# Post-norm linear attention and butterfly FFN on one core: the last three x chunks transposed in another PSUM bank, three more layer norms applied by ScalarE

## Chip, core, metric

One core of a Trainium2 chip. The time is device microseconds of the one core, median of 3 runs; lower is better. The engines are named as in the profile: PE (TensorE), PEld (its weight loads), DVE (VectorE), ACT (ScalarE), POOL (GpSimd), SP (the queue that issues the DMAs).

## What is computed

Input x is 4 sequences of 1024 tokens with 128 features, float32. One transformer block in post-norm form:

```python
def layernorm(x): return (x - mean(x)) / sqrt(var(x) + 1e-5)
def fmap(t): return relu(t @ W_f + b_f)            # per head, 64x64
q, k, v = split(x @ W_qkv)                         # 16 heads of 64
q, k = fmap(q), fmap(k)
kv = einsum('bhnd,bhne->bhde', k, v)
att = einsum('bhnd,bhde->bhne', q, kv) / (einsum('bhnd,bhd->bhn', q, k.sum(n)) + 1e-6)
x = layernorm(x + att.merge_heads() @ W_out + b_out)
h = butterfly(x @ W_exp + b_exp, up_weights)       # 512 hidden, 9 stages
h = butterfly(gelu(h + up_bias), down_weights)
x = layernorm(x + h @ W_con + b_con + down_bias)
```

## The kernel before

**Tiling.** The tokens form 8 chunks n of 512 (two per sequence b, c = 0 or 1) and 32 tiles of 128 tokens. Heads go in 8 pairs of 128 features. The butterflies are linear, so they are multiplied into the weights once: the up butterfly by POOL, the down butterfly by DVE in nine steps (`down_step`, slots 1 to 10). Matrix products in fp32r are made of three, from a high and a low part of each operand (`split`, L600): ACT writes the high part (`hi`, L936), DVE the low one (`lo`, L1135).

**Order.** It is written by hand as a loop over 43 slots, the same loop on each engine. One slot in steady state, on PE: a key tile for half the heads (`project_k(kt, 0)`), one pair of attention (`add_attn`), a query step of 128 features by 512 tokens (`project_q`), the other half of the keys, a second `add_attn`, the product of keys and x (`add_kx`, L678), a second `project_q`, and now and then something more. PE in slot s uses for `add_attn` what DVE (`normalise_q`, L1267, then `qn_lo`) and ACT (`qn_hi`) made in slot s - 1. From slot 28 (NO_KEYS) no key tiles are left. Each engine takes its instructions strictly in turn and waits only on counters (semaphores) of the others.

**PSUM.** Eight banks. Three (`ring`) go round among projections, denominators (`norm`), the FFN's `up` and `down` tiles: a use waits until the use three before it has been drained. Two hold `kx_ps`, one `attn_ps`. The last two matter here. `desk` takes everything that is transposed (chunks of x: `transpose_x`; of the attention: `transpose_attn`; of the first layer norm's result: `transpose_x1`; of the FFN's result: `transpose_y`; weights) and the small products `ksum` and `head_maps`. It has one user at a time: `desk_of` numbers the uses, and PE waits with `take_desk` until the one before was read (`s_dtaken`). `spare_ps` serves the weight folding and down butterfly steps 3 to 7, is last read by step 8 in slot 10, and then is empty until the last chunk's halves in the tail (`spare_of`, `take_half`).

**x transposes.** `XT_SLOT` puts x of sequence 1 in slots 2 and 6, of sequence 2 in 10 and 14, of sequence 3 in 18 and 22, at the slot's end. ACT copies the high part from `desk` at once (`xT_hi`). DVE takes a row sum and the low part only in the next slot (`xT_lo`, L1309 and L1135), after that slot's first key drain (`k_max(kt, 0)`, L1207) and two `normalise_q`. Then come `k_sum`, `qn_lo`, `k_max(kt, 1)`, and where there is one `add_x` (L1292: attention from `desk` plus x, then statistics) or `residual` (L1301: FFN plus x1), and a second `qn_lo`. In slots 15, 19, 23, 27, ... PE transposes an attention chunk in `desk` after the slot's first `project_q`; in slots 17, 19, 25, 27, 33, 35 it ends with `head_maps` in `desk`; in slots 16, 20, 24, ... it ends with `transpose_x1`, which waits for `s_x1`.

**Layer norms.** DVE makes mean and variance, POOL adds eps and takes the power -1/2 (`rstd_of`). Then there are two ways, chosen by the slot against NO_KEYS = 28. In an earlier slot POOL also makes an offset (two more operations), and ACT applies the norm in the next slot, four activations of 128x128 (`layer_norm_apply`, L1004), between the first query copy and the second `qn_hi`. From slot 28 on DVE waits for POOL and applies it itself, four operations (`layer_norm_end`, L1285), at the end of the same slot. The first layer norm of chunk n has its statistics in slot 15 + 4n, the second of chunks 0 to 3 in slots 22, 26, 30 and 34.

```python
dve.wait_ge(s_rs[i], n + 1)                       # layer_norm_end, DVE
act.wait_ge(s_of[i], 2 * n + 2)                   # layer_norm_apply, ACT
take_desk: pe.wait_ge(s_dtaken, desk_of[use])     # PE, before any use of desk
```

Of the kernel before, what the change touches and what calls it, by code (L numbers as in the profile page):

```python
# [5 lines left out]
def postln_linear_attention_butterfly_ffn_kernel(  # L6
# [123 lines left out]


# [45 lines left out]
    for s in range(SLOTS):  # L177
        order = []
        if s in KSUM_SLOT:
            order.append(("ksum", KSUM_SLOT[s]))  # L180
        if s in ATT_T_SLOT:
            order.append(("attn", ATT_T_SLOT[s]))
        if s in YT_SLOT:
            order.append(("y", YT_SLOT[s]))
        if s in MAPS_SLOT:
            order.append(("maps", *MAPS_SLOT[s]))
        if s == BIAS_T_SLOT:
            order.append(("bias",))
# [11 lines left out]
    spare_of = {("attn", LAST, 1): 0, ("x1", LAST, 1): 1, ("y", LAST, 1): 2}  # L200
# [5 lines left out]
    with ctx:  # L206
# [190 lines left out]
        def half_bank(use):  # L397
            return desk if use[2] == 0 else spare_ps

        def half_made(use):  # L400

            return (s_dmade, desk_of[use] + 1) if use[2] == 0 else (s_smade, spare_of[use] + 1)

        def half_taken(use):
            return (s_dtaken, desk_of[use] + 1) if use[2] == 0 else (s_staken, spare_of[use] + 1)
# [107 lines left out]
        def _(pool):  # L513
# [55 lines left out]
            for s in range(SLOTS):  # L569
# [25 lines left out]
        def _(pe):  # L595
# [23 lines left out]

            def transpose_weights(grp, dst):  # L620
# [258 lines left out]
            def take_half(use):  # L879
                if use[2] == 0:  # L880
                    pe.wait_ge(s_dtaken, desk_of[use])
                elif spare_of[use]:
                    pe.wait_ge(s_staken, spare_of[use])
                else:

                    pe.wait_ge(s_dn, 3 * STAGES)

# [40 lines left out]
        def _(act):  # L928
# [47 lines left out]
            def xT_hi(b, c):  # L976
                act.wait_ge(s_dmade, desk_of["x", b, c] + 1)
# [3 lines left out]
                hi(xT_h[:, b % 2, c * CH:(c + 1) * CH], desk[:, :], s_xTh)  # L981
# [57 lines left out]
            for s in range(SLOTS):  # L1039
# [91 lines left out]
        def _(dve):  # L1131
# [203 lines left out]
            for s in range(SLOTS):  # L1335
# [140 lines left out]
```

## Time and profile before

| | us |
|---|---|
| three timed runs | 342.19, 343.95, 344.32 (median 343.95) |
| the profiled execution | 346.04 |
| its span, first to last instruction | 344.1 |
| busy in it: PE | 314.7 (91%) |
| DVE | 249.2 (72%) |
| ACT | 154.9 (45%) |
| POOL | 84.4 (25%) |

Times in rows are microseconds from the span's start in the profiled execution. A timeline row gives start, duration, engine, line, operation, the tile written and those read, and in brackets how long the engine sat idle before and whose work ended that. Matmuls are pipelined: a matmul of 512 columns is shown for 0.39 us and the next begins 0.23 us after it did, so in a row of matmuls the starts are what counts. Of the span outside the instructions nothing is shown; it is the 1.9 us between 346.04 and 344.1.

### The profile page before, as it was taken

To read this page: it belongs to the slowest core of one execution; us is meant where nothing else is said; L and a number is where in the kernel's file an instruction comes from. 1 tells how busy PE (TensorE), PEld (TensorE's weight loads), DVE (VectorE), ACT (ScalarE), POOL (GpSimd) and SP (SyncE) were. 2 spreads that over 40 slices of the span, in tenths; PEclk is the share of its full clock that TensorE was granted. 3 is DMA by queue.
4 is the path that set the end of the run, shared out by engine and by line. 5 is a ranking of instruction groups with operands and counts; after the bars stand their busy time and mean duration, and the time that the engine had idled before them with its cause. 6 is when DMAs were issued, how large, how long until landed. Compare 5 with 4: busy or idle time off the path is not lost.

```text
span 344.1 us, 5110 instructions
## 1 busy us (share of the span) xinstructions
PE 314.7 (91%) x1813; PEld 218.5 (64%) x1813; DVE 249.2 (72%) x492; ACT 154.9 (45%) x272; POOL 84.4 (25%) x94
## 2 busy tenths in 40 slices
PE   5799799999989979997999889999999798989882
PEld 5666476776757756665767667567778556554562
DVE  3569999969599988678681986489647837577555
ACT  3533235444534433544452546356746553341451
POOL 4059999950000002100200220004001101111122
PEclk9999899999999999999999999999999999999998
DMA  5994153835701900720073003800290074641002
GB/s 184 253 294 137 61 183 124 250 120 127 181 2 50 199 0 4 182 65 0 5 167 80 0 3 93 185 0 2 56 225 3 3 174 105 164 116 30 21 10 61
DMA packets 25616, 33.72 MB, mean 98 GB/s; under 512 B 4184, under 2 KB 14456, under 8 KB 25592
## 3 DMA queue, kind: packets, MB, share of 16 engines
q1 hardware_dynamic: 25432, 33.38, 37.4%
q8 instruction: 14, 0.23, 0.3%
q14 instruction: 10, 0.08, 0.1%
q10 hardware_dynamic: 160, 0.03, 0.0%
HBM read 31.04 MB, written 2.36 MB: 97 GB/s over the span
## 4 chain that ended last, share of the span: by engine, by line
PE 71%; DVE 14%; DMA 5%; issue 4%; SPq 3%; POOL 2%; ACT 1%; POOLq 0%; DVEq 0%; ACTq 0%
PE ring L600 25%; PE kx_ps L678 12%; PE attn_ps L600 7%; PE ring L774 6%; PE ring L698 4%; PE desk L609 4%; PE attn_ps L728 4%; DVE qn L1267 3%; DMA x<-_L_ffn_down_weights_dram 2%; PE desk L712 2%; DMA bf_col<-in_L_attn_b_f_dram 2%; PE desk L687 2%; DVE late L1153 2%; PE ring L658 2%; SPq L474 1%
## 5 line engine op out<-in xcount | busy, mean ns | idle before, releaser
L950 ACT ACTIVATE q<-ring,bf_col 128x512 f32<-128x512 f32 x64 | 43.7, 685 | 51.2 <-PE ring L600 50.7
L552 POOL TENSOR_TENSOR var_eps<-mean_var,ln_eps 128x4 f32<-128x4 f32 x14 | 7.1, 504 | 222.7 <-DVE mean_var L1280 222.7
L678 PE MATMUL kx_ps<-k,xs 128*128 128x512 f32 x128 | 60.1, 592 | 0.0
L936 ACT ACTIVATE qn_h<-qn 128x512 fp32r<-128x512 f32 x48 | 29.6, 625 | 32.6 <-DVE qn L1267 32.6
L1267 DVE TENSOR_TENSOR qn<-q,recips 128x512 f32<-128x512 f32 x64 | 41.1, 681 | 4.3 <-DMA recips<-recip_rows 4.3
L544 POOL TENSOR_TENSOR y<-hid,y_up 128x512 f32<-128x512 f32 x18 | 34.6, 1946 | 16.9 <-DMA hid<-in_L_ffn_up_weights_dram 15.9
L1135 DVE TENSOR_TENSOR qn_l<-qn,qn_h 128x512 fp32r<-128x512 f32 x48 | 32.2, 678 | 5.2 <-ACT qn_h L936 5.0
L1207 DVE TENSOR_TENSOR k<-ring,bf_minus 128x512 f32<-128x512 f32 x32 | 21.9, 685 | 19.1 <-PE ring L600 19.1
L600 PE MATMUL ring<-xT_h,wq_h 128*128 128x512 f32 x64 | 35.5, 555 | 0.1
L1233 DVE TENSOR_TENSOR k_total<-k_total,k 128x1024 f32<-128x1024 f32 x24 | 35.3, 1472 | 0.3
L678 PEld LDWEIGHTS kx_ps<-k,xs 128*128 128x128 f32 x128 | 23.9, 189 | 17.8 <-issue 15.4
L600 PE MATMUL ring<-wk_h,xT_h 128*128 128x512 f32 x64 | 29.6, 462 | 0.0
L943 ACT ACTIVATE k<-ring 128x512 f32<-128x512 f32 x32 | 19.1, 598 | 20.0 <-PE ring L658 20.0
L600 PE MATMUL ring<-wk_l,xT_h 128*128 128x512 f32 x64 | 25.4, 397 | 0.0
L774 PE MATMUL ring<-hid,wdn 128*128 128x512 f32 x56 | 25.4, 596 | 0.0
L600 PE MATMUL ring<-wk_h,xT_l 128*128 128x512 f32 x64 | 25.4, 396 | 0.0
L600 PE MATMUL ring<-xT_h,wq_l 128*128 128x512 f32 x64 | 25.2, 394 | 0.0
L600 PE MATMUL ring<-xT_l,wq_h 128*128 128x512 f32 x64 | 25.1, 392 | 0.0
L1013 ACT ACTIVATE hid<-ring,bup_col 128x512 f32<-128x512 f32 x28 | 19.2, 686 | 8.9 <-PE ring L600 8.8
L600 PE MATMUL attn_ps<-qn_h,m_h 128*128 128x512 f32 x48 | 20.0, 418 | 1.1 <-DVE qn_l L1135 1.1
L600 PE MATMUL attn_ps<-qn_h,m_l 128*128 128x512 f32 x48 | 18.9, 393 | 0.0
L600 PE MATMUL attn_ps<-qn_l,m_h 128*128 128x512 f32 x48 | 18.7, 391 | 0.0
(171 smaller groups left out, 573.8 us busy)
## 6 DMA issues: line engine op xcount, KB each, us to landing
recips<-recip_rows SPq DMA_DIRECT2D x64, 256.0 KB, 5.0
hid<-in_L_ffn_up_weights_dram SPq DMA_DIRECT2D x9, 512.0 KB, 4.6
x<-_L_ffn_down_weights_dram SPq DMA_DIRECT2D x9, 512.0 KB, 3.8
xs<-in_L_attn_x_dram SPq DMA_DIRECT2D x4, 512.0 KB, 6.8
out_dram<-y SPq DMA_DIRECT2D x7, 256.0 KB, 4.2
q<-in_L_attn_W_qkv_dram SPq DMA_DIRECT2D x2, 512.0 KB, 8.8
q<-in_L_attn_W_qkv_dram SPq DMA_DIRECT2D x2, 256.0 KB, 3.0
q<-in_L_attn_W_out_dram SPq DMA_DIRECT2D x2, 256.0 KB, 9.2
```

Source lines behind the costliest of these rows:

```text
L544: g.tensor_tensor(term_up[f].rearrange("p (hi j lo) -> p hi j lo", j=2, lo=lo), w[:, :, :, :, f], yv[:, :, f:f + 1, :].to_broadcast([128, ...
L600: last = t_.matmul(dst, lhsT, rhs, start=start and n == 0, stop=stop and n == len(pairs) - 1)
L678: t_.matmul(kx_ps[half], xs[b % XBUF][:, t, :], k[kt % KRING][:, half * CH:(half + 1) * CH], start=t == 0, stop=t == TILES - 1).then_inc(s ...
L774: last = t_.matmul(bank(("down", n))[:, :], wdn[:, i, :], hid[:, i, :], start=i == 0, stop=i == HT - 1)
L936: a_.activation(dst, src, ACT.Copy).then_inc(done, 1)
L943: a_.activation(k[kt % KRING][:, half * CH:(half + 1) * CH], bank(("k", kt, half))[:, :], ACT.Relu).then_inc(s_taken, 1)
L950: a_.activation(q[:, i % QRING, :], bank(("q", i))[:, :], ACT.Relu, bias=bf_col[:, :])\
L1013: a_.activation(hid[:, i, :], bank(("up", f))[:, :], ACT.Gelu, bias=bup_col[:, i:i + 1])\
L1135: v.tensor_tensor(dst, src, high.bitcast(fp32), ALU.subtract).then_inc(done, 1)
L1207: v.tensor_tensor(k[kt % KRING][:, half * CH:(half + 1) * CH].rearrange("p (h d) -> p h d", d=D), bank(("k", kt, half))[:, :].rearrange("p ...
L1233: v.tensor_tensor(k_total[:, :], k_total[:, :], k[kt % KRING][:, :], ALU.add).then_inc(s_ks, 1)
L1267: v.tensor_tensor(qn[:, a % NRING, :], q[:, a % QRING, :], recips[:, a % PAIRS // RC, a % RC, :], ALU.mult).then_inc(s_qn, 1)
```

## The change

Two parts, in one diff.

**Banks.** The transposes of x in slots 14, 18 and 22 (sequence 2's second chunk and both of sequence 3) go to `spare_ps`. They leave `desk_of`, and head `spare_of`, before the three halves of the last chunk. `half_bank`, `half_made` and `half_taken` choose by membership in `spare_of`; `take_half` moves up in the text; the first use of `spare_ps` waits for the down butterfly's last step (27 counts of `s_dn`), each later one for the reader before it. No instruction is added or dropped.

**Layer norms.** `APPLY_END = 35` takes the place of NO_KEYS: the second layer norms of chunks 2 and 3 (slots 30 and 34) and the first of chunk 4 (slot 31) now have their offset from POOL and are applied by ACT in slots 31, 35 and 32. And the two apply calls move, in every slot that has one, to behind the last `qn_hi`.

```diff
+    APPLY_END = 35
...
-        if s in XT_SLOT:
+        if s in XT_SLOT and s <= max(DOWN_STEP_SLOT):
             order.append(("x", *XT_SLOT[s]))
...
-    spare_of = {("attn", LAST, 1): 0, ("x1", LAST, 1): 1, ("y", LAST, 1): 2}
+    spare_of = {}
+    for use in [*[("x", *XT_SLOT[s]) for s in XT_SLOT if s > max(DOWN_STEP_SLOT)],
+                ("attn", LAST, 1), ("x1", LAST, 1), ("y", LAST, 1)]:
+        spare_of[use] = len(spare_of)
...
-            return desk if use[2] == 0 else spare_ps
+            return spare_ps if use in spare_of else desk
...
-                    rstd_of(0, ATT_T_SLOT[s], s < NO_KEYS)
+                    rstd_of(0, ATT_T_SLOT[s], s < APPLY_END)
...
-                    rstd_of(1, YT_SLOT[s], s < NO_KEYS)
+                    rstd_of(1, YT_SLOT[s], s < APPLY_END)
...
+            def take_half(use):
+                if use not in spare_of:
+                    pe.wait_ge(s_dtaken, desk_of[use])
+                elif spare_of[use]:
+                    pe.wait_ge(s_staken, spare_of[use])
+                else:
+
+                    pe.wait_ge(s_dn, 3 * STAGES)
...
             def transpose_x(b, c):
-                take_desk(("x", b, c))
+                use = ("x", b, c)
+                take_half(use)
                 pe.wait_ge(s_xs[b], 16)
-                transpose_tiles(desk, lambda i: xs[b % XBUF][:, QUADS * c + i, :]).then_inc(s_dmade, 1)
+                transpose_tiles(half_bank(use), lambda i: xs[b % XBUF][:, QUADS * c + i, :])\
+                    .then_inc(half_made(use)[0], 1)
...
-                if s <= NO_KEYS and s - 1 in ATT_T_SLOT:
-                    layer_norm_apply(0, ATT_T_SLOT[s - 1], x1[:, ATT_T_SLOT[s - 1] % X1BUF, :, :], s_x1)
-                if s <= NO_KEYS and s - 1 in YT_SLOT:
-                    layer_norm_apply(1, YT_SLOT[s - 1], y[:, YT_SLOT[s - 1] % 2, :, :], s_yo)
...
                 for a in split_spreads(s)[1:]:
                     qn_hi(a)
+                if s <= APPLY_END and s - 1 in ATT_T_SLOT:
+                    layer_norm_apply(0, ATT_T_SLOT[s - 1], x1[:, ATT_T_SLOT[s - 1] % X1BUF, :, :], s_x1)
+                if s <= APPLY_END and s - 1 in YT_SLOT:
+                    layer_norm_apply(1, YT_SLOT[s - 1], y[:, YT_SLOT[s - 1] % 2, :, :], s_yo)
...
-                if s in ATT_T_SLOT and s >= NO_KEYS:
+                if s in ATT_T_SLOT and s >= APPLY_END:
                     layer_norm_end(0, ATT_T_SLOT[s], x1[:, ATT_T_SLOT[s] % X1BUF, :, :], s_x1)
-                if s in YT_SLOT and s >= NO_KEYS:
+                if s in YT_SLOT and s >= APPLY_END:
                     layer_norm_end(1, YT_SLOT[s], y[:, YT_SLOT[s] % 2, :, :], s_yo)
```

`xT_hi`, `xT_lo` and `project_k` read the bank and the counters through the same three helpers.

PE, last rows of slot 14 and the first of slot 15, before (`xs` is x as loaded, `late` the finished attention; slot 18 to 19 and slot 22 to 23 read likewise):

```order
L609 MATMUL desk<-ident,xs 128x128 [waits xs_2_loaded,desk_taken]
L609 MATMUL desk<-ident,xs 128x128 x3
L600 MATMUL ring<-wk_h,xT_h 128x512 [waits ring_bank_taken]
L600 MATMUL ring<-wk_l,xT_h 128x512
L600 MATMUL ring<-wk_h,xT_l 128x512
L600 MATMUL attn_ps<-qn_h,m_h 128x512 [waits qn_lo,qn_hi,attn_copied]
L600 MATMUL attn_ps<-qn_l,m_h 128x512
L600 MATMUL attn_ps<-qn_h,m_l 128x512
L600 MATMUL ring<-xT_h,wq_h 128x512 [waits ring_bank_of_bare_k_taken]
L600 MATMUL ring<-xT_l,wq_h 128x512
L600 MATMUL ring<-xT_h,wq_l 128x512
L609 MATMUL desk<-ident,late 128x128 [waits attn_copied,desk_taken]
```

And with the change:

```order
L614 MATMUL spare_ps<-ident,xs 128x128 [waits xs_2_loaded,down_butterfly]
L614 MATMUL spare_ps<-ident,xs 128x128 x3
L605 MATMUL ring<-wk_h,xT_h 128x512 [waits ring_bank_taken]
L605 MATMUL ring<-wk_l,xT_h 128x512
L605 MATMUL ring<-wk_h,xT_l 128x512
L605 MATMUL attn_ps<-qn_h,m_h 128x512 [waits qn_lo,qn_hi,attn_copied]
L605 MATMUL attn_ps<-qn_l,m_h 128x512
L605 MATMUL attn_ps<-qn_h,m_l 128x512
L605 MATMUL ring<-xT_h,wq_h 128x512 [waits ring_bank_of_bare_k_taken]
L605 MATMUL ring<-xT_l,wq_h 128x512
L605 MATMUL ring<-xT_h,wq_l 128x512
L614 MATMUL desk<-ident,late 128x128 [waits attn_copied,desk_taken]
```

The x transposes write `spare_ps` and wait for the down butterfly; the attention's transposes stand where they stood and still wait for `desk_taken`, whose last count is now that of the bias column.

ACT, slots 31 and 32, before (first row: query copies of slot 31; `hid` the gelu of an `up` tile, `recip` the denominators of `norm`):

```order
L950 ACTIVATE q<-ring,bf_col 128x512 [waits qn_done,ring_bank_made] x2
L936 ACTIVATE qn_h<-qn 128x512 [waits attn_step_added,qn_done] x2
L1013 ACTIVATE hid<-ring,bup_col 128x512 [waits ring_bank_made]
L987 ACTIVATE recip<-ring 128x128 [waits recip_stored,ring_bank_made]
L950 ACTIVATE q<-ring,bf_col 128x512 [waits qn_done,ring_bank_made] x2
L936 ACTIVATE qn_h<-qn 128x512 [waits attn_step_added,qn_done] x2
L1013 ACTIVATE hid<-ring,bup_col 128x512 [waits ring_bank_made]
L936 ACTIVATE x1T_h<-desk 128x512 [waits ring_bank_made,desk_made]
```

And with the change (`y` is the second layer norm of chunk 2, `x` the first of chunk 4):

```order
L957 ACTIVATE q<-ring,bf_col 128x512 [waits qn_done,ring_bank_made] x2
L943 ACTIVATE qn_h<-qn 128x512 [waits attn_step_added,qn_done] x2
L1011 ACTIVATE y<-y,offset,rstd 128x128 [waits offset_1_done]
L1011 ACTIVATE y<-y,offset,rstd 128x128 x3
L1020 ACTIVATE hid<-ring,bup_col 128x512 [waits ring_bank_made]
L994 ACTIVATE recip<-ring 128x128 [waits recip_stored,ring_bank_made]
L957 ACTIVATE q<-ring,bf_col 128x512 [waits qn_done,ring_bank_made] x2
L943 ACTIVATE qn_h<-qn 128x512 [waits attn_step_added,qn_done] x2
L1011 ACTIVATE x<-x,offset,rstd 128x128 [waits offset_0_done]
L1011 ACTIVATE x<-x,offset,rstd 128x128 x3
L1020 ACTIVATE hid<-ring,bup_col 128x512 [waits ring_bank_made]
L943 ACTIVATE x1T_h<-desk 128x512 [waits ring_bank_made,desk_made]
```

Each slot has four activations more. The gelu that frees a ring bank stands behind those of `y`, and `x1T_h` behind those of `x`.

DVE, from the last `qn_l` of slot 30 to that of slot 31, before:

```order
L1135 TENSOR_TENSOR qn_l<-qn,qn_h 128x512 [waits qn_hi]
L1285 TENSOR_SCALAR y<-y,mean_var,rstd 128x128 [waits rstd_1_done]
L1285 TENSOR_SCALAR y<-y,mean_var,rstd 128x128 x3
L1267 TENSOR_TENSOR qn<-q,recips 128x512 [waits qn_lo,qn_hi,recips_of_pairs_2_loaded]
L1267 TENSOR_TENSOR qn<-q,recips 128x512 [waits qn_lo,qn_hi]
L1135 TENSOR_TENSOR qn_l<-qn,qn_h 128x512 [waits qn_hi]
L1292 TENSOR_TENSOR x<-desk,xs 128x512 [waits desk_made]
L1276 BN_STATS stats<-x 128x6 [waits desk_taken]
L1276 BN_STATS stats<-x 128x6 x3
L1278 MEMSET scratch 128x1 [waits stats_0_done]
L1280 BN_AGGR mean_var<-stats 128x2 x4
L1135 TENSOR_TENSOR qn_l<-qn,qn_h 128x512 [waits qn_hi]
```

And with the change:

```order
L1142 TENSOR_TENSOR qn_l<-qn,qn_h 128x512 [waits qn_hi]
L1274 TENSOR_TENSOR qn<-q,recips 128x512 [waits qn_lo,qn_hi,recips_of_pairs_2_loaded]
L1274 TENSOR_TENSOR qn<-q,recips 128x512 [waits qn_lo,qn_hi]
L1142 TENSOR_TENSOR qn_l<-qn,qn_h 128x512 [waits qn_hi]
L1299 TENSOR_TENSOR x<-desk,xs 128x512 [waits desk_made]
L1283 BN_STATS stats<-x 128x6 [waits desk_taken]
L1283 BN_STATS stats<-x 128x6 x3
L1285 MEMSET scratch 128x1 [waits stats_0_done]
L1287 BN_AGGR mean_var<-stats 128x2 x4
L1142 TENSOR_TENSOR qn_l<-qn,qn_h 128x512 [waits qn_hi]
```

The group of four that waited for POOL (`rstd_1_done`) is gone, and `qn` follows the last `qn_l` of the slot before directly. At the end of slots 31 and 34 such a group of four goes as well.

## Rows read from the trace of the kernel before

**Rows 1.** The page: busy us, share of the span, instructions.

```profile
PE 314.7 (91%) x1813; PEld 218.5 (64%) x1813; DVE 249.2 (72%) x492; ACT 154.9 (45%) x272; POOL 84.4 (25%) x94
```

**Rows 2.** Waits: who waited for whom: us in total, times, longest us.

```profile
PE desk L609 <- DVE xT_l L1135: 5.4, 3, 1.8
```

**Rows 3.** Timeline of PE, end of slot 14 to slot 15, and in slot 19.

```profile
122.52 0.66 PE L609 MATMUL desk<-ident,xs 128*128 128x128 f32 x4 [0.26 <-DVE y_bias L1179]
...
124.86 0.40 PE L600 MATMUL ring<-xT_h,wq_l 128*128 128x512 f32 x1
127.06 0.66 PE L609 MATMUL desk<-ident,late 128*128 128x128 f32 x4 [1.80 <-DVE xT_l L1135]
...
160.23 0.66 PE L609 MATMUL desk<-ident,late 128*128 128x128 f32 x4 [1.80 <-DVE xT_l L1135]
```

**Rows 4.** Timeline of DVE: last down step; slot 16; `add_x`, slot 19; second key drain, slot 23.

```profile
94.58 0.69 DVE L1157 TENSOR_TENSOR x<-late 128x512 f32<-128x512 f32 x1
...
132.25 0.69 DVE L1207 TENSOR_TENSOR k<-ring,bf_minus 128x512 f32<-128x512 f32 x1 [0.42 <-PE ring L600]
...
162.43 0.68 DVE L1292 TENSOR_TENSOR x<-desk,xs 128x512 f32<-128x512 f32 x1
...
200.37 0.68 DVE L1207 TENSOR_TENSOR k<-ring,bf_minus 128x512 f32<-128x512 f32 x1
```

**Rows 5.** Timeline of PE: `head_maps` of slot 19, first key tile of slot 24.

```profile
164.61 1.10 PE L712 MATMUL desk<-vo,kx 128*64 128x128 f32 x16
...
203.75 0.39 PE L600 MATMUL ring<-wk_h,xT_h 128*128 128x512 f32 x1
```

**Rows 6.** Timeline of PE, slot 28 (first row) and slots 31 to 33.

```profile
247.20 0.60 PE L609 MATMUL desk<-ident,x 128*128 128x128 f32 x4
...
269.26 0.47 PE L600 MATMUL attn_ps<-qn_h,m_h 128*128 128x512 f32 x1 [0.48 <-DVE qn_l L1135]
...
271.55 0.63 PE L609 MATMUL desk<-ident,x 128*128 128x128 f32 x4 [0.67 <-DVE x L1285]
...
274.16 0.47 PE L600 MATMUL attn_ps<-qn_h,m_h 128*128 128x512 f32 x1 [0.60 <-DVE qn_l L1135]
...
276.47 1.09 PE L712 MATMUL desk<-vo,kx 128*64 128x128 f32 x16 [0.67 <-DVE x1T_l L1135]
```

**Rows 7.** Timeline of DVE, slots 30 to 31.

```profile
261.67 0.66 DVE L1135 TENSOR_TENSOR qn_l<-qn,qn_h 128x512 fp32r<-128x512 f32 x1
263.51 1.11 DVE L1285 TENSOR_SCALAR y<-y,mean_var,rstd 128x128 f32<-128x128 f32 x4 [1.18 <-POOL rstd L558]
264.54 1.28 DVE L1267 TENSOR_TENSOR qn<-q,recips 128x512 f32<-128x512 f32 x2
```

**Rows 8.** Timeline of ACT: layer norm apply in slot 28; slots 31 and 32.

```profile
244.73 1.63 ACT L1004 ACTIVATE x<-x,offset,rstd 128x128 f32<-128x128 f32 x4
...
266.39 0.67 ACT L1013 ACTIVATE hid<-ring,bup_col 128x512 f32<-128x512 f32 x1
...
268.12 0.69 ACT L950 ACTIVATE q<-ring,bf_col 128x512 f32<-128x512 f32 x1 [0.31 <-PE ring L600]
```

**Rows 9.** Timeline of POOL: a layer norm in slot 19, one in slot 27, the starts in slots 30, 31.

```profile
164.51 0.56 POOL L552 TENSOR_TENSOR var_eps<-mean_var,ln_eps 128x4 f32<-128x4 f32 x1 [22.20 <-DVE mean_var L1280]
...
166.33 0.20 POOL L563 TENSOR_TENSOR offset<-mean_minus,rstd 128x4 f32<-128x4 f32 x1
...
238.87 0.55 POOL L552 TENSOR_TENSOR var_eps<-mean_var,ln_eps 128x4 f32<-128x4 f32 x1 [4.88 <-DVE mean_var L1280]
...
241.57 0.20 POOL L563 TENSOR_TENSOR offset<-mean_minus,rstd 128x4 f32<-128x4 f32 x1
...
261.83 0.55 POOL L552 TENSOR_TENSOR var_eps<-mean_var,ln_eps 128x4 f32<-128x4 f32 x1 [20.06 <-DVE mean_var L1280]
...
268.62 0.55 POOL L552 TENSOR_TENSOR var_eps<-mean_var,ln_eps 128x4 f32<-128x4 f32 x1 [5.14 <-DVE mean_var L1280]
```

**Rows 10.** Timeline of PE, the denominators of slot 35.

```profile
288.00 1.96 PE L698 MATMUL ring<-q,ksum_cols 128*32 128x128 f32 x64 [0.87 <-ACT q L950]
```

More of the change, by code:

```diff
@@ L397, in half_bank @@
         def half_bank(use):
-            return desk if use[2] == 0 else spare_ps
+            return spare_ps if use in spare_of else desk
         def half_made(use):
-            return (s_dmade, desk_of[use] + 1) if use[2] == 0 else (s_smade, spare_of[use] + 1)
+            return (s_smade, spare_of[use] + 1) if use in spare_of else (s_dmade, desk_of[use] + 1)
         def half_taken(use):
-            return (s_dtaken, desk_of[use] + 1) if use[2] == 0 else (s_staken, spare_of[use] + 1)
+            return (s_staken, spare_of[use] + 1) if use in spare_of else (s_dtaken, desk_of[use] + 1)
         block = ctx.enter_context(nc.Block())
@@ L643, in project_k @@
                     if b:
-                        pe.wait_ge(s_dtaken, desk_of["x", b, t // QUADS] + 1)
+                        pe.wait_ge(*half_taken(("x", b, t // QUADS)))
                     else:
@@ L877, in _ @@
                     transpose_x1(X1T_SLOT[s])
[L879 to L886, printed above, removed]
             def transpose_half(use, src):
@@ L976, in xT_hi @@
             def xT_hi(b, c):
-                act.wait_ge(s_dmade, desk_of["x", b, c] + 1)
+                act.wait_ge(*half_made(("x", b, c)))
                 if b > 1:
                     act.wait_ge(s_made, ring_of["q", STEPS * (b - 2) + PAIRS * (c + 1) - 1] + 1)
-                hi(xT_h[:, b % 2, c * CH:(c + 1) * CH], desk[:, :], s_xTh)
+                hi(xT_h[:, b % 2, c * CH:(c + 1) * CH], half_bank(("x", b, c))[:, :], s_xTh)
             def norm_eps(n):
@@ L1307, in xT_lo @@
                 dve.wait_ge(s_xTh, CHUNKS * b + c + 1)
+                src = half_bank(("x", b, c))[:, :]
                 if TILES * b >= BARE:
-                    v.reduce_sum(x_part[:, b, c:c + 1], desk[:, :], axis=mybir.AxisListType.X).then_inc(s_xpart, 1)
-                lo(xT_l[:, b % 2, c * CH:(c + 1) * CH], desk[:, :], xT_h[:, b % 2, c * CH:(c + 1) * CH], s_dtaken)
+                    v.reduce_sum(x_part[:, b, c:c + 1], src, axis=mybir.AxisListType.X).then_inc(s_xpart, 1)
+                lo(xT_l[:, b % 2, c * CH:(c + 1) * CH], src, xT_h[:, b % 2, c * CH:(c + 1) * CH],
+                   half_taken(("x", b, c))[0])
             def x1T_lo(n):
```

## Prediction

> **What bounds the kernel now.** I read the page first. PE is busy for 91% of the span, the next engine, DVE, for 72% [rows 1]: PE sets the end, and a stall is worth what PE does not do in it. Then the waits, for those of PE alone: the largest behind the start-up is `desk` waiting for `xT_l`, 5.4 us in three times of 1.8 [rows 2]. Then PE's timeline at these places. After the first query step of slot 15 the attention's transposes begin at 127.06, and the last matmul before began at 124.86; matmuls follow at 0.23 us, so PE lost 127.06 - 124.86 - 0.23 = 1.97 us [rows 3]. That is the idle time shown, 1.80, plus the 0.17 by which a matmul's shown end lies beyond the point where the next could start. Slot 19 is the same (160.23), and slot 23 is the third. The x chunk that slot 14, 18 or 22 left in `desk` waits for DVE, which reads it only after a key drain and two `qn`. Last the timeline of slots 28 to 35, where DVE applies the norms: four gaps of 0.48, 0.67, 0.60 and 0.67 in slots 31 to 33 [rows 6], each with 0.17 more, so 3.1 us in all, and one of 0.87 in slot 35 [rows 10].
>
> **Banks.** (a) Slot 14: x no longer waits for the bias column's reader, 0.26 shown [rows 3], 0.4 with the hidden part. Its new wait, the last down step, ends at 94.58 + 0.69 = 95.3 [rows 4], 27 us before PE is there: nothing.
>
> (b) Slots 15, 19 and 23: the waits for `xT_l` go, 1.97 each, for the previous use of `desk` is then read long before. What is late next is DVE. In these slots it does not stop, and its work is not shorter. It is behind PE by its own backlog, so I look at each later point where PE needs it.
>
> Slot 15: the backlog ends with slot 16's key drain, for which DVE waited 0.42 us [rows 4]. PE being 1.97 + 0.4 earlier, DVE reaches that drain about 2 us late by PE's measure, but the ring's bank is needed only three uses on, and slot 16 has no `desk` use until its end. Slot 15 keeps 2.0, and slot 14 its 0.4.
>
> Slot 19: `head_maps` wants `desk` at 164.61 [rows 5], by PE's own work 1.97 + 0.05 earlier, 162.6 (0.05: matmuls after a gap start a little slower). The bank is then held by the attention that DVE adds at 162.43 for 0.68, up to 163.11 [rows 4]; with 0.06 for the signal, 163.17. PE waits 0.6 again: 1.4 is left. This is a new wait, `desk` for L1292.
>
> Slot 23: the first bank that DVE holds is that of `k_max(kt, 1)`, free at 200.37 + 0.68 = 201.05 [rows 4]; PE wants it for the first key tile of slot 24, 203.75 [rows 5] less 2.0 = 201.75. It clears by 0.7 us: 2.0.
>
> Sum of the banks: 0.4 + 2.0 + 1.4 + 2.0 = 5.8 us. Bounds: if the same 0.6, or DVE's whole backlog up to 1.1 us, came back in slots 15 and 23 too, 3.6; if slot 19 lost nothing, 6.4.
>
> **The order of ACT.** In slots 16, 20, 24 and 28 `x1` is done one `qn_h` later, 0.6 us. The tightest is slot 28: the apply began at 244.73 and took 1.63 [rows 8], so it ended at 246.36, and will at 246.97; PE transposes from 247.20 on [rows 6]. It clears by 0.2: nothing, at worst 0.6. DVE's second `qn_l` no longer waits behind the apply, which no PE instruction is waiting for: nothing.
>
> **Layer norms.** DVE drops per norm four operations (1.11 - 0.08 overlap = 1.03) and the wait for POOL, 1.18: `qn` of slot 31 starts at 264.54 - 2.21 = 262.33, right behind the `qn_l` of 261.67 [rows 7]; slot 32 starts 4.4 earlier. ACT gets 1.6 us per norm, POOL two small operations. What becomes of PE's four gaps goes step by step.
>
> POOL's whole chain with the offset took 166.33 + 0.20 - 164.51 = 2.0 us in slot 19, where DVE sat idle, but 241.57 + 0.20 - 238.87 = 2.9 us at the end of slot 27 [rows 9], where two `qn` came right behind, as they now will in slots 30 and 31. I take 2.9.
>
> Slot 31: the offset of `y` is there at 261.83 + 2.9 = 264.7 [rows 9]. ACT has made both `qn_h` by then (two `qn` of 0.64 from 262.33 on, a copy behind each), applies `y` from 264.7 to 266.4, and only then takes the gelu, which before began at 266.39 [rows 8]: so the bank that this gelu frees is no earlier, and PE's second query step of slot 32 stays where it was. ACT copies it at 268.12 as before [rows 8], done at 268.7, then the two `qn_h` (0.57 each) to 269.9, then `x1` to 271.5. Its offset, at 268.62 - 2.3 + 2.9 = 269.2 [rows 9], is in time. PE wants `x1` at 271.55 less the gap of 0.65 before 269.26, and less its own 0.83: at 270.1 it is there and waits 1.4 us, to 271.5. So of the first two gaps nothing is left, at most 0.35 with POOL's 2.0 (then the gelu ends 0.5 earlier). This is the largest new wait: `desk` for ACT's L1011, where before it was for L1285.
>
> Slot 33: the second two gaps, 0.77 + 0.84 = 1.6, were DVE's lateness (`qn_l` at 274.16, `x1T_l` at 276.47, [rows 6]). DVE being 4.4 us earlier, `qn_l` is done by 270.5, and `x1T_l`, bound by ACT's copy of `x1`, at 273.3, while PE arrives at 274.8. They go: 1.6.
>
> Slots 34 and 35: PE's gap of 0.87 waits for ACT's copy of PE's own last query step [rows 10], and the apply of `y` stands behind that: stays. DVE's 2.2 us there are hidden by its own wait for the denominators: nothing.
>
> Sum of the norms: 1.6, up to 2.0; take 1.7. Bounds: 0.6 and 3.1 (all four gaps).
>
> **A rule against it.** The chain of 2.9 beside 2.0 us [rows 9] is the one place where an added operation meets a neighbour. The Trainium skill (SBUF — State Buffer, Who interferes with whom) says that a DVE operation with two SBUF inputs and a GpSimd operation that reads SBUF block each other, the later for the whole of the other. The rows agree in direction, with 0.9 us for two `qn`; by the rule at its worst each of the three later POOL operations could wait out one. The estimate by it would be a chain of 3.8 us, `y` and with it the gelu 0.9 later, and a total of 6.6 us in place of 7.5.
>
> **Forecast.** 5.8 + 1.7 = 7.5 us. The profiled execution takes 346.04 (344.1 span, 1.94 around it, which the change doesn't touch), so it would take 338.5. The median of the runs is 343.95, 2.1 less, and where that lies no row says; none of the gaps depends on it, so I take off the same: 343.95 - 7.5 = 336.4 us. The timed runs lie 2 us apart.
>
> **Rivals.**
> 1. *DVE's backlog takes the banks' gain back.* For it: DVE is nearly without a pause in slots 15, 19 and 23, and slot 19 shows how it happens. Against: the two other places clear by 0.7 us or more. Each time 1.1 back (the larger of what slot 19 loses and DVE's backlog): 5.8 - 2.2 = 3.6, plus 1.7: 338.7.
> 2. *ACT is not in the way.* The offset comes in 2.0 us, the gelu frees its bank early, and all four gaps and slot 19's 0.6 go: 6.4 + 3.1 = 9.5, 334.4. Against: the two `qn_h` stand before the apply in ACT's row whatever POOL does.
> 3. *Part of the gaps was no loss.* PE runs ahead into the next wait (denominators, query copies by ACT) and only the norms or only the banks count: 343.95 - 1.7 = 342.2 at the least, 338.1 for the banks alone. Nothing in the rows holds PE elsewhere for 5 us.
> 4. *Slower.* The place is `x1_done`: it now comes behind both `qn_h` in slots 16, 20, 24, 28 and 32, and everything of the FFN hangs on it. If ACT started its second `qn_h` only once DVE, late in the slot, had made `qn`, PE would wait in each for what the order costs, 0.6, plus the apply, 1.6: 5 x 2.2 = 11 us lost against at most 7.5 gained, 347.4. It decides from 1.5 us per slot on. Against: slot 28, the tightest, clears by 0.2, and nowhere does `x1_done` stand in the list of PE's waits before slot 32.
>
> **Chances.** Forecast 0.66; rival 1 0.14; rival 2 0.09; rival 3 0.08 (half of it near 338, half within 1%); rival 4 0.03. A measurement of this kernel tells about 1% (3.4 us) from no change. Faster by over 1%: 0.66 + 0.14 + 0.09 + 0.04 = 0.93; within 1%: 0.04 plus 0.01 of rival 4's smaller forms, 0.05; slower: 0.02. The range runs from rival 2 to beyond rival 1, with a microsecond for the runs' scatter: 334.0 to 339.8.
>
> **What would show it.** Right: no wait of PE for `xT_l` in slots 15, 19 and 23; one of about 0.4 us shown (0.6 by starts) for L1292 before `head_maps` in slot 19; one of some 1.2 us for ACT's apply at the end of slot 32; no gap before the first attention of slot 33 or `head_maps` there; ACT's gelu of slot 31 behind the apply; a span of 336 to 337. Wrong: PE waits for `k_max` or `qn_l` in slots 16, 20 or 24; a wait for the apply in slots 16 to 28; POOL's chain above 3 us; PE as long idle as before under other names.

## The result and the profile after

| | before | with the change |
|---|---|---|
| median of the runs, us | 344.13 (342.19 to 345.81, 4 runs) | 335.31 (335.18 to 335.69, 4 runs) |
| profiled execution; its span | 346.04; 344.1 | 335.18; 333.3 |

The changed kernel takes 0.9747 of the time, 95% interval 0.9695 to 0.98: faster, 1.1 us below the forecast of 336.4 and inside its range.

The page of the changed kernel answers to [rows 1]:

```profile
PE 312.0 (94%) x1813; PEld 218.1 (65%) x1813; DVE 242.5 (73%) x480; ACT 160.1 (48%) x284; POOL 88.0 (26%) x100
```

DVE has lost the 12 operations of three norms, ACT has 12 more (5.2 us), POOL six. Of the 6.7 us that DVE is busy for less, the norms are 3.3 (its norm operations took 8.9 us before and 5.6 after); about as much is the difference between two executions, for a second trace of the kernel before has 245.7 us in place of 249.2. PE does the same 1813 matmuls and is idle for less.

PE's waits of the changed kernel, answering to [rows 2] (who waited for whom, us in total, times, longest):

```profile
PE desk L614 <- ACT x L1011: 1.4, 1, 1.4
PE desk L726 <- DVE xT_l L1142: 1.4, 1, 1.4
...
PE desk L726 <- DVE x L1299: 0.5, 1, 0.5
```

The 5.4 us for `xT_l` are gone (the 1.4 left is slot 11's, the first row of the next fence but one). Both new waits are the ones forecast: ACT's apply ahead of slot 32's transposes (1.4 us for some 1.2), and `add_x` ahead of slot 19's `head_maps` (0.5 for about 0.4).

To see where the time went I take the start of the same PE instruction in both traces. PE's timeline of the kernel before, at slots 11, 16, 27 and 36 (the other places are in [rows 5], [rows 6] and [rows 10]):

```profile
99.32 1.09 PE L712 MATMUL desk<-vo,kx 128*64 128x128 f32 x16 [1.22 <-DVE xT_l L1135]
...
132.39 1.95 PE L698 MATMUL ring<-q,ksum_cols 128*32 128x128 f32 x64 [0.17 <-ACT q L950]
...
227.44 0.66 PE L609 MATMUL desk<-ident,late 128*128 128x128 f32 x4 [0.53 <-DVE m_l L1135]
...
302.07 0.66 PE L609 MATMUL desk<-ident,late 128*128 128x128 f32 x4 [0.69 <-DVE x1T_l L1135]
```

The same instructions with the change, those of slots 19, 24, 32 and 35, and the attention's transposes of slots 15 and 23, which start without a wait now:

```profile
96.05 1.09 PE L726 MATMUL desk<-vo,kx 128*64 128x128 f32 x16 [1.36 <-DVE xT_l L1142]
...
121.49 0.60 PE L614 MATMUL desk<-ident,late 128*128 128x128 f32 x4
...
126.76 1.95 PE L712 MATMUL ring<-q,ksum_cols 128*32 128x128 f32 x64 [0.17 <-ACT q L957]
...
157.53 1.09 PE L726 MATMUL desk<-vo,kx 128*64 128x128 f32 x16 [0.49 <-DVE x L1299]
...
189.69 0.60 PE L614 MATMUL desk<-ident,late 128*128 128x128 f32 x4
...
194.62 0.39 PE L605 MATMUL ring<-wk_h,xT_h 128*128 128x512 f32 x1
...
218.30 0.66 PE L614 MATMUL desk<-ident,late 128*128 128x128 f32 x4 [0.52 <-DVE m_l L1142]
...
262.32 0.63 PE L614 MATMUL desk<-ident,x 128*128 128x128 f32 x4 [1.39 <-ACT x L1011]
...
277.17 1.96 PE L712 MATMUL ring<-q,ksum_cols 128*32 128x128 f32 x64 [0.87 <-ACT q L957]
...
291.25 0.66 PE L614 MATMUL desk<-ident,late 128*128 128x128 f32 x4 [0.69 <-DVE x1T_l L1142]
```

| up to | before | after | gained in this stretch | forecast |
|---|---|---|---|---|
| slot 11, `head_maps` | 99.32 | 96.05 | 3.27 | nothing: not edited |
| slot 16, denominators | 132.39 | 126.76 | 2.36 | 2.4 |
| slot 19, `head_maps` | 164.61 | 157.53 | 1.45 | 1.4 |
| slot 27, transposes | 227.44 | 218.30 | 2.06 | 2.0 |
| slot 32, transposes of x1 | 271.55 | 262.32 | 0.09 | 0 to 0.35 |
| slot 35, denominators | 288.00 | 277.17 | 1.60 | 1.6 |
| slot 36, transposes | 302.07 | 291.25 | -0.01 | 0 |

From slot 11's `head_maps` to the end of the span it is 344.1 - 99.32 = 244.78 before and 333.3 - 96.05 = 237.25 after: 7.5 us, the forecast's sum. The 3.27 us ahead of it come from the opening, which the change does not touch. They are why one of the signs named in the prediction was missed, the span of 336 to 337: it was 333.3, and the profiled execution took 335.18 where 338.5 was forecast, 3.3 less. I call this distance "the stretch" below; it is the better scale for small effects, as the experiments show.

### The profile page after: what moved, and what is told of

Same layout as the page of the kernel before. It is cut to its first block, busy times and chain, and to the rows that moved or that the text cites. A ratio compares the mean times of both kernels' runs of the same rounds, so it can differ in the third digit from the quotient of the medians.

```text
span 333.3 us, 5119 instructions
## 1 busy us (share of the span) xinstructions
PE 312.0 (94%) x1813; PEld 218.1 (65%) x1813; DVE 242.5 (73%) x480; ACT 160.1 (48%) x284; POOL 88.0 (26%) x100
## 3 DMA queue, kind: packets, MB, share of 16 engines
HBM read 31.04 MB, written 2.36 MB: 100 GB/s over the span
## 4 chain that ended last, share of the span: by engine, by line
PE 74%; DVE 12%; DMA 4%; issue 4%; ACT 2%; SPq 2%; POOL 1%; POOLq 0%; DVEq 0%; ACTq 0%
PE ring L605 26%; PE kx_ps L692 12%; PE attn_ps L605 8%; PE ring L790 6%; PE ring L712 4%; PE attn_ps L742 4%; PE desk L614 3%; DMA x<-_L_ffn_down_weights_dram 2%; PE desk L726 2%; PE desk L701 2%; DVE qn L1274 2%; PE ring L672 1%; SPq L479 1%; DVE late L1160 1%; DMA q<-in_L_attn_W_qkv_dram 1%
## 5 line engine op out<-in xcount | busy, mean ns | idle before, releaser
L549 POOL TENSOR_TENSOR y<-hid,y_up 128x512 f32<-128x512 f32 x18 | 33.7, 1891 | 16.4 <-DMA hid<-in_L_ffn_up_weights_dram 15.4
```

Source lines behind the costliest of these rows:

```text
L549: g.tensor_tensor(term_up[f].rearrange("p (hi j lo) -> p hi j lo", j=2, lo=lo), w[:, :, :, :, f], yv[:, :, f:f + 1, :].to_broadcast([128, ...
```

## The experiments

Each kernel is the changed one with the edit shown, except the first. Ratios are to the kernel before, run beside it.

**1. Kernel before again.** No edit.

> The kernel before once more, unchanged, for its opening. In the profiled executions the changed kernel reached its first head_maps (slot 11) 3.3 us earlier than the kernel before (96.05 against 99.32), though the change edits nothing ahead of slot 14. Theory: the opening scatters by some 3 us from execution to execution with the landing of the first loads, so this execution reaches that point anywhere between 95 and 100, the ratio is 1.00, and from there to the end it takes 344.1 - 99.3 = 244.8 us, within 0.3. Rival: something in the changed kernel makes its opening shorter; then this one is at 99.3 again, within 0.5.

Measured: 343.69 us (342.16 to 345.95, 10 runs), ratio 1.002 (0.9987 to 1.0052). Its slot 11 `head_maps` starts at 95.68 where the first trace had 99.32, and its stretch is 244.82 against 244.78. So the opening varies by 3.6 us among executions of one kernel, while the stretch agrees within 0.04.

**2. Banks alone.**

```diff
-    APPLY_END = 35
+    APPLY_END = NO_KEYS
...
+                if s <= APPLY_END and s - 1 in ATT_T_SLOT:
+                    layer_norm_apply(0, ATT_T_SLOT[s - 1], x1[:, ATT_T_SLOT[s - 1] % X1BUF, :, :], s_x1)
+                if s <= APPLY_END and s - 1 in YT_SLOT:
+                    layer_norm_apply(1, YT_SLOT[s - 1], y[:, YT_SLOT[s - 1] % 2, :, :], s_yo)
                 for kt in k_tiles(s)[:1]:
...
                 for a in split_spreads(s)[1:]:
                     qn_hi(a)
-                if s <= APPLY_END and s - 1 in ATT_T_SLOT:
...
```

The applies go back ahead of the second `qn_hi`.

> Only the three x transposes go to the empty bank; layer norms as before, in number and in place. Theory: from slot 11's head_maps on, the gain over the kernel before is 0.4 + 2.0 + 1.4 + 2.0 = 5.8 us, so 1.6 to 1.7 us slower than the changed kernel (337.0); PE waits for add_x before head_maps of slot 19 (0.5 shown), and shows the old four gaps in slots 31 to 33. Rival, DVE's backlog: without the relief of DVE more of the 5.8 comes back in slots 15 to 24, gain under 4.5.

Measured: 337.21 us (336.42 to 339.05, 4 runs), ratio 0.9826 (0.9775 to 0.9877); stretch 238.93, a gain of 5.85 where 5.8 was forecast. PE waits 0.5 us for `add_x` ahead of slot 19's `head_maps`, and its old four gaps in slots 31 to 33 (0.48 to 0.67 us before) are all there.

**3. Norms alone**, with the new order on ACT and x in `desk`.

```diff
-        if s in XT_SLOT and s <= max(DOWN_STEP_SLOT):
+        if s in XT_SLOT:
...
-    for use in [*[("x", *XT_SLOT[s]) for s in XT_SLOT if s > max(DOWN_STEP_SLOT)],
-                ("attn", LAST, 1), ("x1", LAST, 1), ("y", LAST, 1)]:
+    for use in [("attn", LAST, 1), ("x1", LAST, 1), ("y", LAST, 1)]:
```

> Only the layer norms: up to slot 34 by ACT behind its query copies, x transposes all in desk. Theory: the three waits of 1.8 for xT_l stay, slots 31 to 33 gain 1.6 to 1.7 us over the kernel before, 5.8 us slower than the changed kernel (341.1). Rival: the new order of ACT pays something in slots 16 to 28 as well, then the gain is over 2.2 us.

Measured: 342.1 us (341.12 to 344.93, 10 runs), ratio 0.9977 (0.9944 to 1.001), which by itself would not show a gain; stretch 243.07, a gain of 1.71 where 1.7 was forecast. PE's waits of this kernel:

```profile
PE desk L613 <- DVE xT_l L1141: 5.4, 3, 1.8
...
PE desk L613 <- ACT x L1010: 1.4, 1, 1.4
```

The old wait is whole and the new one for ACT is there. 5.85 + 1.71 = 7.56 against 7.53 together: the parts neither help nor hinder each other.

**4. The applies back ahead of the second `qn_hi`**, the rest as changed: the move shown in experiment 2, with `APPLY_END = 35` kept.

> The changed kernel with the apply calls put back ahead of the second qn_h; banks and APPLY_END = 35 as changed. Theory: slots 16 to 28 do not care (DVE's second qn_l waits up to 1.3 us again, PE for nothing). In slot 31 the apply of y waits for POOL anyway, the second qn_h and the gelu come 0.6 later, and PE's second query step of slot 32 with them, while x1 of slot 32 saves the same 0.6 by going before the second qn_h: x1_done and the total as in the changed kernel, within 0.3 us (335.0 to 335.6). Rival: the order is what makes the norms' move pay, then it is 0.6 to 1.7 us slower.

Measured: 336.29 us (334.88 to 337.89, 4 runs), ratio 0.9793 (0.9739 to 0.9847); stretch 237.20, against 237.25. The order is worth nothing. PE's timeline in slot 32 of this kernel shows why:

```profile
258.93 0.50 PE L605 MATMUL ring<-xT_h,wq_h 128*128 128x512 f32 x1 [0.52 <-ACT hid L1020]
...
262.82 0.63 PE L614 MATMUL desk<-ident,x 128*128 128x128 f32 x4 [0.87 <-ACT x L1011]
```

0.52 + 0.87 = 1.39 is the single wait of the changed kernel, in two pieces: ACT's work up to the end of the apply is the same in either order.

**5. Chunk 4's x1 norm back on DVE**, so that of the three moved norms ACT applies only the second ones of chunks 2 and 3.

```diff
-                    rstd_of(0, ATT_T_SLOT[s], s < APPLY_END)
+                    rstd_of(0, ATT_T_SLOT[s], s < NO_KEYS)
...
-                if s <= APPLY_END and s - 1 in ATT_T_SLOT:
+                if s <= NO_KEYS and s - 1 in ATT_T_SLOT:
...
-                if s in ATT_T_SLOT and s >= APPLY_END:
+                if s in ATT_T_SLOT and s >= NO_KEYS:
```

> The changed kernel, but chunk 4's first layer norm (slot 31) applied by DVE again at the end of its own slot; both second norms stay with ACT. Times from slot 11's head_maps on, where the changed kernel takes 237.25 us. Theory: PE's 1.39 wait for ACT's apply in slot 32 goes (DVE has x1 0.9 us before PE wants it), 1.5 us won; but DVE, 2.2 us later again, makes x1T_l in slot 33 behind two qn, and PE waits for it before head_maps, some 0.9 of it: 0.5 to 0.7 us faster than the changed kernel, 236.6. Rival: DVE is the engine that had to be relieved there; then the old gaps come back and it is 1 us slower or more, 238.3.

Measured: 337.23 us (334.6 to 337.92, 4 runs), ratio 0.9802 (0.9731 to 0.9872); stretch 236.70, 0.55 better than the changed kernel. The median alone would say the opposite (335.31 for the changed kernel); in this trace slot 11's `head_maps` started only at 99.20, 3.15 us later than with the change. The wait for ACT is gone and one for DVE is back one slot later:

```profile
268.23 1.09 PE L726 MATMUL desk<-vo,kx 128*64 128x128 f32 x16 [0.67 <-DVE x1T_l L1142]
```

**6. Slot 19's `k_sum` behind `add_x`.**

```diff
+                late_sum = s == 19
                 for kt in kx_tiles(s):
-                    if kt % TILES:
+                    if kt % TILES and not late_sum:
                         k_sum(kt)
...
                     add_x(ATT_T_SLOT[s])
+                if late_sum:
+                    for kt in kx_tiles(s):
+                        k_sum(kt)
```

> The changed kernel, with slot 19's k_sum (1.2 us) moved on DVE from before qn_lo to behind add_x, so that desk is read 1.1 us earlier. Theory: the new wait of PE for L1299 before head_maps in slot 19 (0.49 shown, 0.6 by starts) goes and nothing takes its place: 236.6 from slot 11's head_maps on, against 237.25. Rival: DVE's backlog shows at the next place (key drain or qn_l of slot 20), no gain.

Measured: 335.72 us (334.49 to 337.32, 4 runs), ratio 0.9765 (0.9684 to 0.9845); stretch 236.68, 0.57 better. `head_maps` of slot 19 no longer waits:

```profile
159.21 1.09 PE L726 MATMUL desk<-vo,kx 128*64 128x128 f32 x16
```

**7. More work for DVE** in slots 11, 15, 19 and 23: a second row sum of x into a tile that nobody reads.

```diff
+                    v.reduce_sum(x_more[:, 2 * b + c:2 * b + c + 1], src, axis=mybir.AxisListType.X)
                     v.reduce_sum(x_part[:, b, c:c + 1], src, axis=mybir.AxisListType.X).then_inc(s_xpart, 1)
```

> The changed kernel with one more row reduction of the x chunk (0.6 us on DVE, result unused) ahead of each of the four in slots 11, 15, 19 and 23: DVE's backlog made longer at the places in question. Theory: slot 11 pays 0.6 (there PE already waits for xT_l), slot 19 pays 0.6 (add_x later), slot 15 nothing, slot 23 nothing or at most 0.1, its bank clearing by 0.7: from the end of slot 11's wait on 0.6 slower than the changed kernel, 237.9. Rival: DVE bounds PE in all of these slots; then 1.8 slower, 239.1.

Measured: 338.27 us (336.65 to 339.49, 4 runs), ratio 0.9843 (0.9777 to 0.9909); stretch 238.54, 1.3 worse. PE's timeline, slots 19 and 24, and between them DVE's key drain of slot 23, here:

```profile
158.49 1.09 PE L727 MATMUL desk<-vo,kx 128*64 128x128 f32 x16 [1.08 <-DVE x L1300]
...
195.75 0.47 PE L606 MATMUL ring<-wk_h,xT_h 128*128 128x512 f32 x1
```

```profile
194.93 0.68 DVE L1215 TENSOR_TENSOR k<-ring,bf_minus 128x512 f32<-128x512 f32 x1
```

Slot 19 pays in full, 1.08 - 0.49 = 0.59. Slot 23's drain ends at 195.61, just ahead of the key tile, which has lost 0.1; the margin is used up. Slot 15 pays nothing (from slot 11's `head_maps` to slot 16's denominators 30.76 us, with the change alone 30.71).

That makes 0.7 of the 1.3 us, and the expectation was 0.6, 237.9. The other 0.6 stand at no wait. PE falls behind the changed kernel at an even pace, and it does so before the first added operation, which DVE starts at 94.34 in slot 11. At the x transposes in slot 2 the two traces are level (36.45 here, 36.47 with the change); the last matmul ahead of the transposes of slot 10 starts here at

```profile
87.68 0.39 PE L606 MATMUL ring<-xT_h,wq_l 128*128 128x512 f32 x1
```

and with the change at

```profile
87.50 0.39 PE L605 MATMUL ring<-xT_h,wq_l 128*128 128x512 f32 x1
```

So PE lost 0.2 us in those 51 us, 0.4%, with the granted clock at 1.00 in both. The same pace over the stretch would be about 0.9 us (an estimate), enough for the 0.6, which need no effect of DVE's backlog. Why the matmuls follow each other more slowly in this trace stays open: the kernel also has one more tile in SBUF, and there is only one trace of it.

**8. The best version:** edits 5 and 6, and in slot 33 `x1T_lo` ahead of the two `qn`.

```diff
+                if s == 33:
+                    x1T_lo(X1T_SLOT[s - 1])
                 for a in spreads(s)[:1]:
                     normalise_q(a)
...
-                if s - 1 in X1T_SLOT:
+                if s - 1 in X1T_SLOT and s != 33:
```

> Both e5 and e6, and in slot 33 DVE makes x1T_l ahead of its two qn. Theory: 0.6 from slot 19, 1.5 from slot 32, and x1T_l of slot 33 is ready by the time PE gets to head_maps: 235.1 to 235.3 from slot 11's head_maps on, a median of 333.2. Rival: qn of slot 33, now 0.6 later, or the denominators' reciprocal ahead of qn_l in slot 32, makes PE wait for qn_l before its first attention of slot 33, and 0.5 to 1 us of it is lost.

Measured: 334.23 us (332.85 to 334.69, 4 runs), ratio 0.9722 (0.966 to 0.9783); stretch 235.28, as expected; the median is 1.0 above the 333.2 expected. PE's timeline has neither of the two waits:

```profile
260.81 0.60 PE L614 MATMUL desk<-ident,x 128*128 128x128 f32 x4
...
264.34 1.09 PE L726 MATMUL desk<-vo,kx 128*64 128x128 f32 x16
```

**9. Changed kernel again, and 11. best version again,** beside each other.

> The changed kernel once more, as the base of the others. Theory: from slot 11's head_maps to the end 237.25 us again, within 0.1; the opening anywhere between 95 and 100, so that its runs scatter by 2 to 3 us like the others' and its median is about 7.6 us below that of the kernel before (335.5), not 8.8. Rival: its runs lie within 0.5 us again, as in the first measurement, and the 1.3 us beyond the sum of the gaps belong to the change.

> The kernel of e8 once more, in the same call as the changed kernel: 2.0 us below it in the median and from slot 11's head_maps on (235.3 against 237.25), with a ratio to the kernel before of 0.972, clear of the changed kernel's only just. Rival: the gain of e8 was the opening's scatter; then no difference.

Measured: changed kernel 335.84 us (333.92 to 337.81, 6 runs), ratio 0.9784 (0.9745 to 0.9824), stretch 237.23; best version 333.81 us (332.67 to 335.59, 6 runs), ratio 0.9734 (0.9698 to 0.9771), stretch 235.33. It beats both kernels, the changed one by 2.0 in the median and 1.9 in the stretch, though the two intervals overlap a little. The narrow 0.5 us of the changed kernel's first four runs was luck.

**10. POOL's chain alone:** in slot 31 DVE waits for POOL's offset before its two `qn`.

```diff
+                if s == 31:
+                    dve.wait_ge(s_of[1], 2 * YT_SLOT[s - 1] + 2)
                 for a in spreads(s)[:1]:
```

> The changed kernel, with DVE held at the start of slot 31 until POOL has the offset of y, so that no qn runs beside POOL's four operations there. Theory (a DVE operation with two SBUF inputs holds POOL up): the chain from var_eps to the end of offset in slot 30 takes 2.0 us instead of 2.9, and in slot 31, where nothing is edited, 2.9 as before. Rival: the length comes from ACT or from the place in the program; then it is 2.9 in both. DVE's qn and ACT's copies come 1.7 us later, so the kernel is up to 1.5 us slower; that is not what it is for.

Measured once: 338.32 us, stretch 238.68. POOL's timeline, first with the change (end of slot 30), then in this kernel (end of slots 30 and 31):

```profile
252.70 0.55 POOL L557 TENSOR_TENSOR var_eps<-mean_var,ln_eps 128x4 f32<-128x4 f32 x1 [20.08 <-DVE mean_var L1287]
253.21 0.65 POOL L560 TENSOR_TENSOR mean_minus<-mean_var,minus_one 128x4 f32<-128x4 f32 x1
253.81 1.45 POOL L563 TENSOR_TENSOR rstd<-var_eps,minus_half 128x4 f32<-128x4 f32 x1
255.41 0.20 POOL L568 TENSOR_TENSOR offset<-mean_minus,rstd 128x4 f32<-128x4 f32 x1
```

```profile
253.34 0.55 POOL L557 TENSOR_TENSOR var_eps<-mean_var,ln_eps 128x4 f32<-128x4 f32 x1 [20.07 <-DVE mean_var L1287]
253.85 0.20 POOL L560 TENSOR_TENSOR mean_minus<-mean_var,minus_one 128x4 f32<-128x4 f32 x1
254.00 1.00 POOL L563 TENSOR_TENSOR rstd<-var_eps,minus_half 128x4 f32<-128x4 f32 x1
255.15 0.20 POOL L568 TENSOR_TENSOR offset<-mean_minus,rstd 128x4 f32<-128x4 f32 x1
...
259.47 0.55 POOL L557 TENSOR_TENSOR var_eps<-mean_var,ln_eps 128x4 f32<-128x4 f32 x1 [4.12 <-DVE mean_var L1287]
259.98 0.64 POOL L560 TENSOR_TENSOR mean_minus<-mean_var,minus_one 128x4 f32<-128x4 f32 x1
260.58 1.46 POOL L563 TENSOR_TENSOR rstd<-var_eps,minus_half 128x4 f32<-128x4 f32 x1
262.18 0.45 POOL L568 TENSOR_TENSOR offset<-mean_minus,rstd 128x4 f32<-128x4 f32 x1
```

DVE in this kernel, at the end of slot 30:

```profile
253.18 0.66 DVE L1142 TENSOR_TENSOR qn_l<-qn,qn_h 128x512 fp32r<-128x512 f32 x1
255.38 1.29 DVE L1274 TENSOR_TENSOR qn<-q,recips 128x512 f32<-128x512 f32 x2 [1.54 <-POOL offset L568]
```

With DVE held behind this `qn_l` the chain of slot 30 takes 255.15 + 0.20 - 253.34 = 2.0 us; with two `qn` beside it, 2.9. In slot 31, where DVE is not held, the two middle operations are slow again, and here the last one too (0.45): 262.18 + 0.45 - 259.47 = 3.2 us, where 2.9 was expected. But the time got longer by 1.4: holding DVE puts `qn_h` behind the wait on ACT, so PE now waits 0.95 for the gelu (with the change it does not wait there) and 1.93 for the apply (1.39).

## Why the prediction was right

**Banks.** Each term came out as worked: slots 14 and 15 2.36 (2.4), slot 19 1.45 (1.4), slot 23 2.06 (2.0). Slot 19's new wait is 0.49 shown and 0.57 by experiment 6, where it was taken out (0.6 forecast). The two places said to clear do. Slot 15 kept its whole gain, as the 2.36 show. DVE's drain in slot 23,

```profile
193.26 0.68 DVE L1214 TENSOR_TENSOR k<-ring,bf_minus 128x512 f32<-128x512 f32 x1
```

ends at 193.94, 0.68 us ahead of the key tile at 194.62 (0.7 forecast). Rival 1, the backlog coming back at all three places, falls by the timeline; experiment 7 shows that it is real as a mechanism and was about 0.7 us away in slot 23: one row sum more (0.67 us) uses it up.

**Norms.** ACT's timeline of the changed kernel, slots 31 and 32, against [rows 8]:

```profile
253.83 1.24 ACT L943 ACTIVATE qn_h<-qn 128x512 fp32r<-128x512 f32 x2 [0.49 <-DVE qn L1274]
255.65 1.65 ACT L1011 ACTIVATE y<-y,offset,rstd 128x128 f32<-128x128 f32 x4 [0.58 <-POOL offset L568]
257.20 0.67 ACT L1020 ACTIVATE hid<-ring,bup_col 128x512 f32<-128x512 f32 x1
...
259.50 1.14 ACT L943 ACTIVATE qn_h<-qn 128x512 fp32r<-128x512 f32 x2
260.55 1.63 ACT L1011 ACTIVATE x<-x,offset,rstd 128x128 f32<-128x128 f32 x4
```

The chain is the one forecast: offset late by POOL's 2.91, then the apply, then the gelu behind it, two `qn_h`, the second apply, PE. PE waits 1.39 + 0.17 = 1.56 where 1.4 was forecast, and the two gaps of slot 33 are gone. Norms alone gave 1.71 for 1.7. Rival 2 (ACT not in the way, 334.4) falls: experiment 5 gets back 0.55 of that wait by taking ACT out, experiment 8 the rest. Rival 3 (part of the gaps no loss) falls by experiments 2 and 3, whose gains add up to the whole. Rival 4 (slower, `x1_done` late) falls by experiment 4: with `x1` done earlier the stretch is the same, and no slot from 16 to 28 has a wait for it.

**ACT's order** was put at nothing, and is nothing (0.05).

**The rule of the Trainium skill** (SBUF — State Buffer, Who interferes with whom) would have made the chain 3.8 us and the total 6.6. The direction is now shown by experiment 10 and not only seen side by side; the size is the trace's 2.9, so the sum by the rows was the one to take. The rule itself holds in these traces: a POOL operation that begins inside such a DVE operation is through only when that one is (next section but one). What the prediction had too large is how often. Of the three later POOL operations in slot 30 two began inside a `qn`, each with 0.6 us of it left, which made them 0.45 longer; the third, `offset`, began while DVE added `x`, which has one input from PSUM, and took 0.20.

**The median.** The one step that was off by more than 0.2 us is the base, "the median of the runs is 343.95, 2.1 less, and where that lies no row says". It lies in the opening, at least in good part (next section but one): the profiled execution before had a slow opening, the one after a quick one. By the medians the change gained 8.8 us in the first measurement (344.13 to 335.31) and 7.0 in the second (342.85 for the kernel before, beside experiment 9, to 335.84), on either side of the 7.5. With an opening that varies by up to 4 us, 335.31 and 335.84 for the same kernel, and 336.4 forecast, differ by less than a few runs can tell; the sum of the stretch, 7.5 for 7.5, is the test of the reasoning.

## What to carry to other kernels

A wait for a shared bank is worth its whole length only where the engine that frees it has nothing else due soon: follow that engine to each next point where the bound engine needs it, and subtract there. When work moves to another engine, look at what stands behind it in that engine's row; here that was a gelu and an x1 norm, and one of the three moved norms was better left. Compare small edits by a distance within the trace that starts after the opening, and check it on two executions of one kernel: here it repeated within 0.05 us where the medians moved by about 0.5. Then look where in that distance the difference arises: in experiment 7 only half of it stood at waits, and the rest had begun before the first edited instruction.

## What the hardware showed beside it

**The opening varies, in two ways.** PE's x transposes of slot 2, which wait for DVE's copy of a weight out of `desk`, start anywhere from 36.18 (best version again) to 38.33 us (kernel before). And in four of the thirteen traces (before, 5, 6, and the changed kernel again) the granted clock fell to half soon after, from 38 to 39.5 us on, for some 3 us. Rows by stretch, columns: stretch, length, busy us of PE, PEld, DVE, ACT, POOL (instructions), granted clock, DMA share, GB/s. The kernel before, then the changed one:

```profile
38.00:42.00 4.00, 3.67 (x12) 3.09 (x12) 4.00 (x3) 1.19 (x2) 3.92 (x3) 0.57 0.00 0
39.00:41.00 2.00, 2.00 (x8) 1.62 (x7) 2.00 (x2) 0.60 (x1) 2.00 (x2) 0.50 0.00 0
```

```profile
38.00:42.00 4.00, 4.00 (x16) 2.60 (x15) 3.96 (x3) 1.53 (x3) 3.92 (x3) 1.00 0.22 55
```

0.50 is the lower of TensorE's two levels, 1.2 of 2.4 GHz. The fall followed a stop of PE, 2.49 us of idle ahead of the row at 38.33:

```profile
38.33 1.12 PE L609 MATMUL desk<-ident,xs 128*128 128x128 f32 x4 [2.49 <-DVE q L1387]
```

From these transposes to slot 11's `head_maps` it took 60.5 to 61.0 us in the four traces and 58.9 to 59.8 in the nine others, so the fall costs some 1.4 us (the difference of the two means). Of the 3.27 us between the first two traces, 38.33 - 36.47 = 1.86 is the later start and 60.99 - 59.58 = 1.41 lies behind it, about what the clock costs. The length of the stop does not decide it alone: with banks alone PE stood still for 2.30 us and kept its clock, and in the changed kernel's second trace 1.96 us came ahead of a fall, in the best version's second trace ahead of none. What decides it stays open.

**Small POOL operations beside DVE.** A 128x4 operation took 0.20 us with DVE still and 0.65 with a 128x512 `qn` beside it, the power 1.00 and 1.45: 0.45 us each. For the chain of four that is 0.9 us of latency, which no busy share shows. What decides is the DVE operation that is under way when POOL's begins. In slot 30 of the changed kernel `mean_minus` ended at 253.21 + 0.65 = 253.86, and the first of the two `qn` (from 253.12, some 0.68 long) at 253.80. Beside a longer operation with two inputs in SBUF the wait is longer, as in slot 19 of experiment 6:

```profile
159.83 1.19 DVE L1240 TENSOR_TENSOR k_total<-k_total,k 128x1024 f32<-128x1024 f32 x1
159.99 1.09 POOL L557 TENSOR_TENSOR var_eps<-mean_var,ln_eps 128x4 f32<-128x4 f32 x1 [21.06 <-DVE mean_var L1287]
```

DVE was through at 161.02, POOL at 161.08. It is so in all thirteen traces: the 250 operations of `var_eps`, `mean_minus` and `offset` that began inside a `qn`, `qn_l` or `k_total` ended 0.05 to 0.07 us behind it, and the 142 others, those beside a key drain or `add_x` (one input from PSUM) among them, took 0.19 or 0.20. The 0.55 us of the first operation of a chain, `var_eps`, is such a wait too, for the `qn_l` that follows the statistics; in experiment 10 it ends at 253.89, behind the `qn_l` that ends at 253.84. So the 2.0 us of that chain still hold 0.35 of it. DVE showed no wait in return: two `qn` took 1.28 us beside POOL in the changed kernel's slot 31 and 1.29 us with POOL done in experiment 10.
